# Gathers of a graph neural network kernel, released in groups of four by TensorE's scores

## The reference

```
h = relu(layernorm(x))
# block 0, GraphSAGE-like: the first S = 25 neighbours of a node, channelwise maximum
idx  = first 25 columns with adj != 0
agg  = max over idx of h[idx]            (and 0, if the node has at most 25 neighbours)
x    = x + relu(concat(h, agg) @ W + b)
# block 1, transformer layer with 8 heads of 16 channels
h    = relu(layernorm(x))
allowed = adj | adj.T | eye
s    = where(allowed, q k.T / 4, -inf);  ctx = softmax(s) @ v
y    = layernorm(h + ctx @ Wo.T + bo);   y = layernorm(y + ffn(y))
x    = x + y
```

## Time and profile before

| | us |
|---|---|
| median of 3 runs | 1903.05 |
| lowest and highest | 1896.24, 1905.88 |
| the profiled execution, its own time | 1908.26 |
| its span, first to last instruction | 1906.5 |
| busy: TensorE, ScalarE, VectorE, GpSimd | 1248.9, 809.9, 777.8, 733.2 |
| mean granted TensorE clock, share of full speed | 0.809 |

### The profile page before, as it was taken

One profiled execution on the slowest core, in us unless ns is written; L12 is line 12 of the kernel. 1 busy time (PEld: TensorE's weight loads), 2 busy tenths in 40 slices (PEclk: granted clock), 3 DMA queues, 4 the chain that ended last, 5 costly groups with the idle time before them and its releaser, 6 DMA issues.

```text
span 1906.5 us, 30090 instructions
## 1 busy us (share of the span) xinstructions
PE 1248.9 (66%) x11425; PEld 491.6 (26%) x11486; DVE 777.8 (41%) x3039; ACT 809.9 (42%) x1032; POOL 733.2 (38%) x743
## 2 busy tenths in 40 slices
PE   0144553676783657596585955867575977899985
PEld 0022210132231223232232312313122322343433
DVE  7566455152580536345360633615330231331323
ACT  1121342263543445274351734525342634678652
POOL 5655335724354435605445142633437043300000
PEclk8567776687896879698786977969686987999997
DMA  7432252322242222412223221422213211210000
GB/s 217 144 87 79 62 141 89 79 84 67 88 140 62 63 81 74 115 58 63 88 100 82 68 79 55 139 63 67 54 35 86 72 30 49 69 64 14 7 7 11
DMA packets 104518, 144.51 MB, mean 76 GB/s; under 512 B 17992, under 2 KB 77136, under 8 KB 104336
## 3 DMA queue, kind: packets, MB, share of 16 engines
q1 hardware_dynamic: 68352, 62.67, 10.6%
q0 software_dynamic: 22816, 44.61, 9.9%
q10 hardware_dynamic: 13168, 34.88, 5.3%
HBM read 124.79 MB, written 12.85 MB: 72 GB/s over the span
## 4 chain that ended last, share of the span: by engine, by line
PE 44%; another core or an unknown queue 21%; ACT 13%; issue 11%; DVE 9%; DMA 1%; DVEq 0%; ACTq 0%
PE sc L1526 14%; ACT probs L1307 11%; PE cb L1546 9%; PE sc L1530 7%; PE m L1616 2%; PE m L1603 2%; PE m L1428 1%; DVE cand L736 1%; PE m L1460 1%; DVE keys L732 1%; PE m L1643 1%; PE sc L1568 1%; PE m L1652 1%; PE m L1614 1%
## 5 line engine op out<-in xcount | busy, mean ns | idle before, releaser
L1307 ACT ACTIVATE probs<-sc 128x1024 f32<-128x1024 f32 x512 | 500.1, 1022 | 733.1 <-remote 494.4
L608 POOL DMA_INDIRECT nb_low<-h_rows,lsorted x474 | 473.6, 999 | 723.5 <-DVEq L911 563.4
L1546 PE MATMUL cb<-probs,va 128*17 128x512 f32 x2048 | 342.1, 645 | 40.7 <-issue 38.4
L1526 PE MATMUL sc<-q_near,k_g 32*128 32x512 f32 x1024 | 162.3, 705 | 132.8 <-ACT probs L1307 110.6
L1526 PE MATMUL sc<-q_far,k_g 32*128 32x512 f32 x1024 | 168.1, 694 | 117.2 <-ACT probs L1307 92.1
L1530 PE MATMUL sc<-barred,negident 32*32 32x512 bf16 x4096 | 166.4, 412 | 74.1 <-issue 71.6
L902 DVE TENSOR_REDUCE agg<-nb_low 128x128 f32<-128x1024 f32 (+6 forms) x64 | 114.1, 1783 | 40.9 <-issue 22.4
L1530 PEld LDWEIGHTS sc<-barred,negident 32*32 32x32 bf16 x4096 | 44.2, 89 | 324.5 <-issue 324.5
L673 DVE BATCH_NORM_STATS2 st<-m 128x6 f32<-128x128 f32 x64 | 14.2, 285 | 256.9 <-PE m L1616 208.5
L736 DVE MAX8 cand<-keys 128x8 f16<-128x128 f16 x512 | 105.3, 278 | 3.8 <-remote 1.7
L1299 ACT ACTIVATE barred<-m 128x512 bf16<-128x512 f32 x128 | 74.3, 606 | 74.1 <-issue 35.0
(11 more groups left out here) (186 smaller groups left out, 1620.1 us busy)
## 6 DMA issues: line engine op xcount, KB each, us to landing
adj_t<-in_adj_dram SPq DMA_DIRECT2D x64, 512.0 KB
adj_m<-in_adj_dram ACTq DMA_DIRECT2D x64, 512.0 KB
nb_low<-h_rows,lsorted POOLq DMA_INDIRECT x474
xh<-in_x_dram SPq DMA_DIRECT2D x8, 512.0 KB
h_rows<-xh SPq DMA_DIRECT2D x8, 512.0 KB
hl<-h_rows SPq DMA_DIRECT2D x8, 512.0 KB
x<-in_x_dram SPq DMA_DIRECT2D x16, 256.0 KB
out_dram<-h2T SPq DMA_DIRECT2D x16, 256.0 KB
```

The lines of the kernel that those rows point to most:

```text
L608: pool.indirect_dma_start(out=dst, out_offset=None, in_=h_rows[0:(f + 1) * (N + 1), :], in_offset=bass.IndirectOffsetOnAxis(ap=lsorted[:, ...
L1307: nc.scalar.activation(probs[:, i % 2, 2 * pair:2 * pair + 2, :], sc[:, 2 * pair:2 * pair + 2, :], ACT.Exp, scale=SCALE).then_inc(s_probs, 1)
L1526: nc.tensor.matmul(sc[:, a, :], k[part, :], q[part, :], start=True, stop=False)
L1546: last = nc.tensor.matmul(cb[a * SPAN:a * SPAN + VW, :], va[:, u % 2, a, kt, :], probs[:, i % 2, a, :], start=(kt == 0), stop=(kt == T - 1))
```

## The change

Every wait is on s_scores, ahead of levels 0, 4, 8, ... of tiles 0 and 1 of graphs 3 to 7. The number waited for is twice a count of steps, so the wait of level k of tile 0 is over when the scores of steps 0 to 12 + k / 4 of slot f - 2 are complete, and that of level k of tile 1 when those of steps 0 to 12 + (k + 18) // 4 are, with at most step 19 asked for.

```diff
+            def paced(f, t, k):
+
+                return 2 * (STEPS * (f - 2) + min(13 + (k + (BASE[0] + 2) * t) // 4, 20))
+
             @block.gpsimd
...
                         for k in range(lo, hi):
+                            if f > AHEAD and t < 2 and k % 4 == 0:
+                                pool.wait_ge(s_scores, paced(f, t, k))
                             if k == lo and k < NA and i >= 2:
                                 pool.wait_ge(s_pooled, i - 1)
                             if k in (lo, NA) and k >= NA and i >= 1:
```

## The result

The changed kernel took 1837.51 us (median of 4 runs, 1830.51 to 1840.10) against 1901.30 us for the kernel before beside it: a ratio of 0.967, with a 95% interval of 0.964 to 0.970.

The account below looks back on a forecast made before the run. The prediction took TensorE nearly standing during long rows of GpSimd gathers to hold the chain. Slot gains 3 + 4.1 + 5.5 + 3.9 + 6.7 = 23.2 us, off the 1903.05 median, gave 1880 us; range 1840 to 1915.

Parts of the forecast that it names:

- The added waits: Some 40 waits on GpSimd, taken at 0; at the worst 0.3 us each and all on the path, 12 us.
- Slot 1: Only tile 1's level 8 waits, for step 18, which comes some 3 us sooner: gain 3 us.
- the price of a group behind a pause: Later gather groups in slots 2 to 5: each costs 1.25 us a gather plus 3.0 us.
- the short run: Six gathers and one store, 944.8 to 953.3 us; second-half scores read as 3.0 us behind the last gather's end.
- 16 gathers and their tail: Slots 2 to 4: first 16 gathers go unbroken at 1.25 us each, then a 5.3 us tail before step 16.
- slot 5, first gather to step 12's scores: Slot 5's run, begun at 1441.4 us, is held for step 12's scores, complete by about 1445.4 us.
- A: Nothing comes of it: TensorE loses time per gather, not per run, and tails refill the pauses; 1903 us, chance 0.20.
- C: Slower: each paced group leaves the full 5.3 us tail, not 3.0; sum +19.6 us, time 1922 us, chance 0.15.
- B: A pause clears everything: steps keep their undisturbed pace behind the first tail; gain 86 us, time 1817 us, chance 0.13.
- Rule against row: Skill's shared-DMA-engines rule alone makes pacing worth 0; the trace has DMA engines under half busy while TensorE stands.

Follow-up runs that it names:

- threes: Changed kernel with waits ahead of every third gather, for steps 12 to 22, in place of every fourth: 1793.41 us, 0.943 of the kernel before; 1312.86 us, 1.000 on another chip.

## Why the prediction was wrong

**The direction and the structure were right.** The stall was put where it is, and the waits met by the time of each run were counted right: sixteen gathers in a row in slots 2 to 4, then 6 or 8, 4 and 3; seven groups in slot 5; in slot 1 only the last three wait. The added waits cost nothing (0.30 us between gathers, as before). The run at step 28 is unchanged: steps 26 to 31 of slot 2 take 45.4 us, where they took 44.8. Slot 1 gained 2.7 us for 3 forecast.

**The step that failed is the price of a group behind a pause**, "a group now costs its gathers plus the 3.0 us of the short run". Measured lags are less than that (us; the forecast of a group of 6 is 7.5 + 3.0, and so on):

| term | forecast | measured | slots |
|---|---|---|---|
| 16 gathers and their tail | 25.3 | 23.0, 23.0, 22.9 | 2, 3, 4 |
| group of 8 | 13.0 | 12.1, 11.8 | 3, 5 |
| group of 6 | 10.5 | 9.2, 8.9 | 2, 4 |
| group of 4 | 8.0 | 5.7 to 6.1 | 2 to 5 |
| group of 3 | 6.75 | 3.1 to 4.6 | 2 to 5 |
| slot 5, first gather to step 12's scores | 4.0 | 0 | 5 |

The lag behind the gathers (1.25 us each) is 0.7 to 1.1 us for four, 1.4 to 1.7 for six, 1.8 to 2.1 for eight and 3.0 for sixteen; before it is 4.9 to 5.1 for 29 and 5.3 to 5.4 for 31. It grows with the length of the row. Two of the intervals, as ScalarE shows them in slot 3 (a row of 8, then one of 4):

```profile
995.51 1.94 ACT L1313 ACTIVATE probs<-sc 128x1024 f32<-128x1024 f32 x2 [15.19 <-remote]
...
1007.57 1.94 ACT L1313 ACTIVATE probs<-sc 128x1024 f32<-128x1024 f32 x2 [8.25 <-remote]
...
1013.57 1.94 ACT L1313 ACTIVATE probs<-sc 128x1024 f32<-128x1024 f32 x2 [3.08 <-PE sc L1536]
```

I took one lag from a single short run for every group, and the lag of a run of 31 for one of 16. And the short run was misread. Its last transfer is not the gather that ends at 951.97 us but the store behind it:

```profile
952.27 0.99 POOL L592 DMA_INDIRECT pooled_rows<-agg,lsorted  x1 [0.30 <-issue]
```

From its end at 953.26 to the second half's 954.84 it is 1.6 us, not 3.0, in line with the 1.4 to 2.1 us of six to eight gathers above. With 1.6 for the sixteen groups the sum of the forecast would be 23.2 + 16 x 1.4 = 45.6 us, an estimate. The kernel before shows the growth too: in slots 2 to 4 the next scores come 1.5 us behind the end of a row of 8 transfers, 3.7 to 4.5 behind one of 21 and 5.1 to 5.5 behind one of 30 to 32. By slots the error is 9.2, 7.5, 8.2 and 17.7 us in slots 2 to 5, less 0.3 in slot 1: 42.3 us, all of the difference of 65.5 and 23.2.

In slot 5 four of its 17.7 us are another term. I took step 12's scores at 1445.4 us from the trace of before, where they were themselves held up by the gathers begun at 1441.4. With the wait ahead of the first gather they are there first: the exponential is at 1389.32, the gather at 1389.64. A time that the removed cause had made late may not be used in the sum.

**The rivals.** A, nothing comes of it, falls by the result: the same number of gathers cost less once they were parted. C, the full tail behind each group, falls by the table. B, a pause clears everything, at 1817 us, came nearer than the forecast (20.5 us off against 42.5) and had the mechanism: between groups the steps of slot 5 go at 6.0 us with four gathers in 5.0. It was too low since a group of six to eight still leaves 1.4 to 2.1 us. The argument that I set against it, that groups would join to one run, is what slots 2 to 4 show for the waits already met, and it isn't so for the later ones, where GpSimd stood 1.0 to 3.7 us at each wait.

**Rule against row.** By the Trainium skill, "DMA: Bandwidth & Descriptors", section "Issuing engines are not separate DMA queues", DMAs of all engines interleave on the same 16 DMA engines. Taken alone, as in the prediction, this has the gathers compete with transfers only and the change worth 0. On the chip where the changed kernel was timed without the stall it is worth 0 (1.000), with DMA engines 0.65 busy beside a full TensorE. On the chips of the stall the measurement decides against it as the whole story: TensorE nearly stands at a share of 0.48.

Instruction fetch, which the prediction named beside rival B, is not what the long stall waits for. The section of the Trainium skill cited there ("Runtime: NRT & Kernel Launch", "Instruction fetch mechanics") has the stall only behind a taken branch whose target isn't in the current window of two pages, a condition that the prediction left out. These are all the queues that moved a packet in the kernel before from 1014 to 1053 us, in which stretch TensorE goes from near standing back to its pace:

```profile
q0 software_dynamic: 641, 1.31, 25.1%
q10 hardware_dynamic: 256, 0.92, 6.8%
```

No packet of an instruction queue is among them, so TensorE came free at 1042 us without one. How long a fetch takes, from the queue rows of the changed kernel, first in the long row of slot 2 (766 to 785 us) on a chip with the stall, then in 694 to 734 us on one without:

```profile
q8 instruction: 1, 0.02, 0.3%
q14 instruction: 2, 0.02, 0.2%
```

```profile
q8 instruction: 4, 0.07, 0.6%
q14 instruction: 1, 0.01, 0.1%
```

One packet of q8 took 0.3% of 16 engines' 19 us, some 0.9 us; four took 0.6% of 40 us, 1.0 us each. Once under way a fetch is about as fast in the stall as outside it.

**What stays open:** what GpSimd's row of transfers holds up in TensorE (from 1003 to 1037 us it started 31 matmuls and 29 weight loads, with the DMA engines half idle), whether its matmuls or their signals are late, and why some chips have it and others not. That parting the gathers helps, and that neither bytes nor the place matter, is shown by the runs; whether the breaks do it or the lower number of gathers in a given time isn't.

## What to carry to other kernels

Where an engine with no wait of its own goes still while GpSimd issues one gather after another, part the row: idle pauses in the gathers of two tiles of five graphs were worth 5 to 6% here, waits for the consumer's steps in the same tiles 3%, and pauses of two microseconds in all tiles 16 to 17%. Count every transfer of a row before taking its lag, price a group by the lag of rows of its own length, not by one lag for all, and never take a start time from a trace in which the cause that you remove had already delayed it. And run the kernel before again beside each version: a gain on one chip (0.943 for threes) was nothing on another (1.000).

## What the runs showed of the hardware that I had not expected

- The kernel before takes 1898.6, 1900.5 and 1900.0 us on three chips, and 1312.7 and 1313.3 on two others (medians). The traces of the changed kernel on either kind have equal durations of each gather (1.00 us), of each exponential (1.02 us) and equal transfers (44.61 MB on the queue of the gathers); steps 13 to 19 take 55.9 us in slot 3 on the one and 29.4 on the other, and 29.4 on both in slot 6, where there are no gathers.
- Fetching half as many bytes with as many transfers, in the gathers of two tiles, left the stall as it was (0.998).
- On the chips of the stall TensorE's finished scores reach ScalarE late: in the kernel before 70 of 512 more than 0.5 us behind the modelled end of their last matmul, 402 us in all; on the others none.
- The lag after a row of gathers grows with its length: 0.7 to 1.1 us after 4, 2 after 8, 3.0 after 16, 5.3 to 5.4 after 31. In all tiles of six graphs, a break of 0.85 us in place of 0.30 cut the whole kernel to 0.935, one of 2.15 us to 0.831 and 0.837.
- Six idle adds on GpSimd, 120 times (184 us of work that computes nothing), took 16 to 17% off the time, where the stall is.
